# Routed expert results in a vision tower: three accumulators in DRAM, or one row per pick and token

## The reference

```python
h = h + _L1_ffn_ref(_layernorm(h, axis=-1), Wg, bg, Wge, bge, W1, b1, W2, b2)

# inside _L1_ffn_ref: G, E = 4, 8 (32 experts); KG, KE = 2, 2 (four picks per token)
comb = _combine_weights(xf, Wg, bg, Wge, bge)          # (tokens, 32), four non-zero each
h = gelu(einsum('nd,edm->nem', xf, W1) + b1)           # M = 768
y = einsum('nem,emd->ned', h, W2) + b2
out = einsum('ne,ned->nd', comb, y)
```

## Time and profile before

| | us |
|---|---|
| median of 3 runs | 1153.36 |
| lowest, highest | 1148.75, 1153.44 |
| the profiled execution | 1146.11 |
| its span, first to last instruction | 1144.3 |
| TensorE matmuls busy in it | 1015.9 |
| VectorE, ScalarE, GpSimd busy | 403.2, 671.7, 232.7 |

### The profile page before, as it was taken

The page is one execution under the profiler, slowest core; times in us unless marked ns, Lnnn a source line. Parts: engine busy times, 40 slices in busy tenths (PEclk is TensorE's granted clock), DMA queues, the critical chain, the costliest instruction groups (busy, mean ns, idle before and its releaser), DMA issues. The chain is left out here.

```text
span 1144.3 us, 22007 instructions
## 1 busy us (share of the span) xinstructions
PE 1015.9 (89%) x7432; PEld 668.2 (58%) x7432; DVE 403.2 (35%) x1027; ACT 671.7 (59%) x1227; POOL 232.7 (20%) x236
## 2 busy tenths in 40 slices
PE   8879689989999999999999998873299999999992
PEld 7455456633444444444445454452189999999992
DVE  2666968750111111111111115767822222222220
ACT  0657957679988888888788852451033433343330
POOL 0110310000000000000000000200655555555532
PEclk9999889989999999999999998896589999999997
DMA  9200037979555445455444401004199999999994
GB/s 278 79 2 0 1 125 262 340 270 172 120 117 134 111 114 127 95 124 124 112 111 117 106 1 46 0 6 129 49 326 313 311 307 306 309 309 307 304 288 73
DMA packets 72411, 183.74 MB, mean 161 GB/s; under 512 B 15712, under 2 KB 30400, under 8 KB 72008
## 3 DMA queue, kind: packets, MB, share of 16 engines
q1 hardware_dynamic: 59260, 166.24, 48.7%
q0 software_dynamic: 12640, 16.16, 7.1%
q10 hardware_dynamic: 432, 0.26, 0.1%
HBM read 147.52 MB, written 36.67 MB: 161 GB/s over the span
## 5 line engine op out<-in xcount | busy, mean ns | idle before, releaser
L1145 ACT ACTIVATE sle_H<-sle_hp 128x1024 f32<-128x1024 f32 x384 | 367.5, 1024 | 61.1 <-PE sle_hp L1082 61.1
L1565 ACT ACTIVATE ext_H<-ext_hp,ext_bias 128x128 f32<-128x128 f32 x378 | 104.3, 375 | 171.9 <-issue 153.8
L1099 PE MATMUL sle_up<-sle_H,sle_cw 128*32 128x512 f32 (+1 forms) x2048 | 193.5, 496 | 0.0
L1523 PE MATMUL ext_yp<-ext_w,ext_H 128*128 128x192 f32 x756 | 139.7, 335 | 2.2 <-ACT ext_H L1565 1.6
L1160 DVE STREAM_TRANSPOSE sle_UT<-sle_up 128x256 f32<-128x256 f32 x64 | 37.3, 583 | 295.1 <-PE sle_up L1099 295.1
L1523 PEld LDWEIGHTS ext_yp<-ext_w,ext_H 128*128 128x128 f32 x756 | 121.1, 190 | 10.0 <-issue 2.6
L1082 PE MATMUL sle_hp<-keep_G,keep_dT 99*128 99x512 bf16 (+1 forms) x512 | 103.6, 337 | 10.9 <-PEq L880 5.7
L1099 PEld LDWEIGHTS sle_up<-sle_H,sle_cw 128*32 128x32 f32 x2048 | 53.8, 109 | 87.6 <-issue 74.2
L1082 PE MATMUL sle_hp<-sle_G,sle_dT 99*128 99x512 bf16 (+1 forms) x512 | 99.9, 327 | 1.1 <-ACT sle_H L1145 1.1
L1067 POOL COPY sle_cw<-keep_CT 128x128 f32 (+1 forms) x64 | 18.7, 293 | 396.1 <-PE sle_up L1099 396.0
L1508 PE MATMUL ext_hp<-ext_xT,ext_w 128*128 128x128 f32 x756 | 96.1, 277 | 0.0
(11 more groups left out here) (258 smaller groups left out, 1158.2 us busy)
## 6 DMA issues: line engine op xcount, KB each, us to landing
ext_w<-W SPq DMA_DIRECT2D x126, 576.0 KB
pieces<-hid_gp SPq DMA_DIRECT2D x16, 1152.0 KB, 4.9
keep_G<-pieces SPq DMA_DIRECT2D x32, 288.0 KB, 3.9
sle_G<-pieces SPq DMA_DIRECT2D x32, 288.0 KB, 3.8
pieces<-hid_gp SPq DMA_DIRECT2D x8, 768.0 KB, 4.7
keep_G<-pieces SPq DMA_DIRECT2D x32, 192.0 KB, 3.8
sle_G<-pieces SPq DMA_DIRECT2D x32, 192.0 KB, 3.7
keep_CT<-xT SPq DMA_DIRECT2D x6, 512.0 KB, 6.2
```

Source lines behind the costliest of these rows:

```text
L1099: mm = pe.matmul(to[32 * e:32 * e + 32], cw[:, p, 2 * e + grp, :], H[:, p, h:h + width], start=(p == 0 and grp == 0), stop=(p == 1 and grp ...
L1145: act.activation(H[:, p, WIDTH * k:WIDTH * (k + 1)], hp[k % DEEP][:].rearrange("p a c -> p (a c)"), ACT.Gelu_apprx_tanh).then_inc(gelu_don ...
L1523: mm = pe.matmul(yp[:, 0:D], H[:, q, c, :], w2[:, q, c, :], start=(c == 0), stop=(c == HC - 1))
L1565: act.activation(H[:, q, c, :], hp[q][:, c % 2, (c // 2) * P:(c // 2 + 1) * P], ACT.Gelu, bias=bias[:, q, c:c + 1]).then_inc(gelu_done, 1)
```

## The change

The three tensors with additions are replaced by one DRAM tensor `chosen` of 4 * 1024 + 128 rows, in which each (pick, token) pair has its own row.

- `route` no longer zeroes `sum1` and `sum2`. `rt.slot` is unchanged, but the third number of it is no longer read.
- SP no longer stores h to `out` at the start.
- Each scatter is plain, goes to `chosen` at the pair's number (`rt.slot[:, 1]`), and waits for the landing of the scatter before it, tile t - 1. All use one semaphore, `y_out`. `leave_y` waits for the same scatter as before, that of tile t - 3, by that semaphore's count.
- The merges go. When all 63 scatters have landed, SP loads `chosen` back in eight pieces, two halves of the tokens by four picks, each 128 x 4 x 192, into `back`. VectorE adds each piece to h, and SP stores each half of h to `out` when its four are added.

```diff
-            sp.wait_ge(zero_ready, 1)
-            for rows in others:
-                sp.dma_start(rows.rearrange("(i p) d -> p i d", p=P), zero[:].unsqueeze(1).to_broadcast([P, TILES + 1, D])).then_inc(zero_out, 16)
...
-            sp.wait_ge(zero_out, 16 * len(others))
...
-            pool.memset(zero[:], 0.0).then_inc(zero_ready, 1)
...
-                if first and p == DEEP - 1:
-                    sp.wait_ge(h_done, TILES // 2)
-                    sp.dma_start(out[0:TOKENS].rearrange("(i p) d -> p i d", p=P), g.h[:]).then_inc(first_out, 16)
-                    sp.dma_start(out[TOKENS:TOKENS + P], g.h[:, 0, :]).then_inc(first_out, 16)
 
             program(sp, load)
+            rows = lambda dram: dram.rearrange("(i p) d -> p i d", p=P)
+            sp.wait_ge(y_out, 16 * MOE_TILES)
+            for half in range(2):
+                at = slice(half * TILES // 2, (half + 1) * TILES // 2)
+                for k in range(TOPK):
+                    sp.dma_start(back[:, k, at], rows(chosen[k * TOKENS:(k + 1) * TOKENS])[:, at]).then_inc(back_in[half][k], 16)
+            for half in range(2):
+                at = slice(half * TILES // 2, (half + 1) * TILES // 2)
+                sp.wait_ge(total, TOPK * (half + 1))
+                sp.dma_start(rows(out[0:TOKENS])[:, at], g.h[:, at]).then_inc(total_out, 16)
+            sp.wait_ge(total_out, 32)
...
-                dve.tensor_copy((xi, yi)[n][q][:], rt.slot[:, 2 * n, bass.ds(t, 1)]).then_inc((xi_ready, yi_ready)[n], 1)
+                dve.tensor_copy((xi, yi)[n][q][:], rt.slot[:, n, bass.ds(t, 1)]).then_inc((xi_ready, yi_ready)[n], 1)
...
-                    dve.wait_ge(y_out[q], 16 * uses(p, r))
+                    dve.wait_ge(y_out, 16 * (t - DEEP + 1))
...
             leave_y(MOE_TILES - 1, BODY - 1, ROUNDS - 1, False)
+            for half in range(2):
+                at = slice(half * TILES // 2, (half + 1) * TILES // 2)
+                for k in range(TOPK):
+                    dve.wait_ge(back_in[half][k], 16)
+                    dve.tensor_tensor(g.h[:, at], g.h[:, at], back[:, k, at], ALU.add).then_inc(total, 1)
+                    dve.wait_ge(total, TOPK * half + k + 1)
...
-            def scatter(t, p, r, first, last):
-                q = p % DEEP
-                to = 0 if last and p >= BODY - DEEP else q
+            def scatter(t, p, start):
                 pool.wait_ge(yi_ready, t + 1)
                 pool.wait_ge(y_done, t + 1)
-                if first:
-                    pool.wait_ge(first_out, 32)
-                else:
-                    pool.wait_ge(y_out[to], 16 * (uses(p, r) + q - to))
+                if not start:
+                    pool.wait_ge(y_out, 16 * t)
                 pool.sem_inc(turn, 1)
-                pool.indirect_dma_start(out=sums[to], out_offset=bass.IndirectOffsetOnAxis(ap=yi[q][:], axis=0),
-                                        in_=y[:, q, :], in_offset=None, compute_op=ALU.add).then_inc(y_out[to], 16)
-
-            def merge(into, q):
-                whole = lambda rows: rows[0:TOKENS].rearrange("(p i) d -> p (i d)", i=4)
-                pool.dma_start(whole(sums[into]), whole(sums[q]), accum_op=ALU.add, max_dma_last_dim=4 * 4 * D).then_inc(merged, 16)
+                pool.indirect_dma_start(out=chosen, out_offset=bass.IndirectOffsetOnAxis(ap=yi[p % DEEP][:], axis=0),
+                                        in_=y[:, p % DEEP, :], in_offset=None).then_inc(y_out, 16)
...
-                    scatter(t - 1, (p - 1) % BODY, r + (p - 1) // BODY, first and p <= DEEP, last and p > 0)
-                if last and p == BODY - DEEP + 1:
-                    for q in range(1, DEEP):
-                        pool.wait_ge(y_out[q], 16 * (MOE_TILES // DEEP - 1))
-                    merge(1, 2)
+                    scatter(t - 1, (p - 1) % BODY, first and p == 1)
 
             for q in range(BODY):
                 gather(q, q)
             program(pool, tile)
-            scatter(MOE_TILES - 1, BODY - 1, ROUNDS - 1, False, True)
-            pool.wait_ge(merged, 16)
-            pool.wait_ge(y_out[0], 16 * (MOE_TILES // DEEP + DEEP - 1))
-            merge(0, 1)
-            pool.wait_ge(merged, 32)
+            scatter(MOE_TILES - 1, BODY - 1, False)
+            pool.wait_ge(y_out, 16 * MOE_TILES)
...
-        others = [nc.dram_tensor(f"sum{i}", (TOKENS + P, D), F32).ap() for i in range(1, 3)]
-        route(nc, g, a, rt, xn_dram, others)
-        expert_tiles(nc, g, a, rt, xn_dram, out, others)
+        chosen = nc.dram_tensor("chosen", (TOPK * TOKENS + P, D), F32).ap()
```

More of the change, by code:

```diff
@@ L1203, with route @@
     pass
-def route(nc, g, a, rt, xn_dram, others):
+def route(nc, g, a, rt, xn_dram):
     SETS = TILES * G1 + TILES
@@ L1231, in route @@
         lg = s.sb("lg", [P, TILES, G1 + EXPERTS])
-        zero = s.sb("zero", [P, D])
         val = s.sb("val", [P, SETS, E1])
@@ L1256, in route @@
                                "in_ready", "step"))
-        zero_ready, zero_out = s.sem("zero_ready"), s.sem("zero_out")
         xn_out, row_ready, owner_ready, owner_out, slot_done, gate_ready, gate_out = (
@@ L1422, in _, with expert_tiles @@
             dve.wait_ge(slot_done, 2)
-def expert_tiles(nc, g, a, rt, xn_dram, out, others):
+def expert_tiles(nc, g, a, rt, xn_dram, out, chosen):
     DEEP, BODY = 3, 9
     ROUNDS = MOE_TILES // BODY
-    sums = [out, *others]
     with Scope(nc, "ext") as s:
@@ L1442, in expert_tiles @@
         shareT = s.sb("shareT", [P, 2, P])
+        back = s.sb("back", [P, TOPK, TILES, D])
         xi = [s.sb(f"xi{i}", [P, 1], U32) for i in range(BODY)]
@@ L1449, in expert_tiles @@
                                "gelu_done", "y_ready", "y_done", "turn", "step"))
-        share_ready, shareT_done, b2_ready, h_done, first_out, merged = (
-            s.sem(n) for n in ("share_ready", "shareT_done", "b2_ready", "h_done", "first_out", "merged"))
-        y_out = [s.sem(f"y_out{i}") for i in range(DEEP)]
+        share_ready, shareT_done, b2_ready, h_done, y_out, total, total_out = (
+            s.sem(n) for n in ("share_ready", "shareT_done", "b2_ready", "h_done", "y_out", "total", "total_out"))
+        back_in = [[s.sem(f"back_in{half}_{k}") for k in range(TOPK)] for half in range(2)]
         w1_in, w2_in = ([s.sem(f"{n}{i}") for i in range(DEEP)] for n in ("w1_in", "w2_in"))
@@ L1683, in routed_moe @@
         xn_dram = nc.dram_tensor("xn", (TOKENS, ROW), F32).ap()
-        others = [nc.dram_tensor(f"sum{i}", (TOKENS + P, D), F32).ap() for i in range(1, 3)]
-        route(nc, g, a, rt, xn_dram, others)
-        expert_tiles(nc, g, a, rt, xn_dram, out, others)
+        chosen = nc.dram_tensor("chosen", (TOPK * TOKENS + P, D), F32).ap()
+        route(nc, g, a, rt, xn_dram)
+        expert_tiles(nc, g, a, rt, xn_dram, out, chosen)
 def build(nc, a, out):
```

## The result

The changed kernel takes 1183.06 us (median of 4 runs, 1174.18 to 1188.97), the kernel before in the same series 1151.05 us (4 runs, 1145.57 to 1153.44). The ratio is 1.028, with a 95% interval from 1.023 to 1.033: slower by 2.8%. The time lies in the forecast's range of 1147 to 1195, but the likeliest case, 1155 and no change, was wrong. It is rival B in its mild form, which stood at 1181. The range reached up to 1195 in order to hold that rival, so the time's place in it says nothing for the mechanism that was forecast.

The account below looks back on a forecast made before the run. TensorE was taken to set the pace, 4.57 us a tile. Loop terms summed to 0 and the end to +1.4 us; on the three runs' median of 1153.36 us that gave 1154.8, rounded 1155, range 1147 to 1195.

Parts of the forecast that it names:

- the likeliest case: Whole kernel: the scatter chain fits the tile period and the ends cancel; 1155 us, from 1152 to 1160, chance 0.46.
- rival B: GpSimd's wait for scatter t-1 binds the tile loop from a landing of 3.70 us on; chances 0.26 mild, 0.12 strong.
- mild form: Tile loop: a landing of 4.1 us makes a loop of 5.0, +26 us, 1181 us; 1160 to 1195, chance 0.26.
- What bounds the kernel: Routed tile loop: TensorE sets the pace at 4.57 us a tile; DMA engines just keep up, cheaper transfers give nothing.
- Zeroing and stores of h: In `route` and at the routed stage's start: removing zeroing is worth 0, removing stores of h 0, at most -1 us.
- The chain: Tile loop: each scatter waits for the one before; landing plus 0.87 against 4.57 us, sum 0, bounds 0 and +134 us.
- a late scatter moves itself: Tile loop: a late scatter slides against weight loads until it falls behind the burst or in the gap, landing in about 3 us.
- The gap: Tile loop: plain scatters leave the DMA engines 0.65 us free in each 4.57 us period, a load of 86%.
- strong form: Tile loop: landing of 5.2 us, loop of 6.1, price 90 us, 1245 us; over 1195, chance 0.12.
- The end: Behind the last matmul: merges go, eight loads, adds and stores come; span ends at 1145.7 against 1144.3, +1.4 us, between -1 and +6.
- The open 4.3 us: End of the span before: 4.3 us after the second merge landed, unexplained; 0.6 taken for the new end, 4.3 kept as bound.
- rival D: End is longer: the eight loads don't run at 317 GB/s, or the 4.3 us stay; 1161 us, chance 0.05 beyond 1159.

Follow-up runs that it names:

- light weights: Changed kernel, chain kept, with half of each W2 left out of its load (down product reads three of six chunks twice): 1156.0 us, one run.

## Why the prediction was right and where it was wrong

**What bounds the kernel: right.** TensorE sets the pace before, and cheaper transfers give nothing in the loop: plain scatters alone leave the period at 4.57 us.

**Zeroing and stores of h: not contradicted.** They were put at 0 and -1 us at most. The 1.06 us less from the first gather to the first `y` is within what that stretch varies by (16.6 to 20.4 us), so these runs can't tell it from 0.

**The chain: the form of the sum was right, the choice of its value was the step that failed.** The loop is landing plus 0.81 us (I had 0.87; outside the hardware loop over the tiles it is 0.88 to 0.90 here too), so it binds from a landing of 3.76 us on, and the scatter and then `leave_y` wait as I had it. The last link was wrong: TensorE waits not for `leave_x` and x transposed but for `leave_y` to free `yp`, before its down product. That changes no number. The bounds, 0 and 134 us, held the 27.3 us. The failed step reads "I take the low part of it, a loop that just fits, for one reason: a late scatter moves itself". What the runs show in its place: a late scatter did move against the weight loads, and settled in no place where it lands in about 3 us. In the changed kernel the first eight loops, while TensorE still kept its own pace, were 4.35 to 7.66 us, 6.0 in the mean; with nine buffers 28 tiles passed that way at 5.9 us a loop. The loop came down to 5.0 us only once TensorE waited for the chain: slower tiles and so fewer weights, perhaps also a fixed order between the two. I didn't have this feedback, and what needs TensorE to wait can't end at 4.57 us. The gap on which I relied was also smaller: 0.09 of a period (share 0.91 without a chain), not 0.14.

I had two rows of landings beside load, 5.21 and 5.9 us, and an idle one of 3.52, and for a loop in which the engines are 86% busy I took a value from the idle end. By the fit of the Trainium skill, in "DMA: Bandwidth & Descriptors" (Anatomy of one DMA), an estimate for this scatter is 2.2 us. The idle rows agree, 2.3 us; in the loop it is 4.2. The same page of the Trainium skill (Latency and other measured facts) has the fixed cost grow with the load of HBM, which was the sentence beside rival B, and the rows go the same way, 2.3 us to 4.2; that HBM is the cause no run here shows.

**Rival B: right in mechanism and, for the loop, in size.** It had a landing of 4.1 us, a loop of 5.0 and 26 us; measured 4.2, 5.0 and 27.3. That its total, 1181, is so near to 1183 is partly luck: it stood on 1153.4 us before, and the end cost 5.3 us more than it held. The reason that kept its strong form unlikely, that slower tiles fill less of the engines, was just the feedback: I used it to cap the loss and not to see that it also holds the loop above the period.

**The end: +1.4 predicted, +6.65 measured.** By its terms:

| term | predicted | measured |
|---|---|---|
| last `y` to the issue of the last scatter | 2.2 | 6.8 |
| its landing | 2.9 | 2.3 |
| the loads, to the last piece in SBUF | 11.7 | 13.3 |
| last add | 1.0 | 1.0 |
| last store | 2.9 | 2.6 |
| block end | 0.6 | 0.4 |

The first is the chain once more, three scatters to drain at 3.21 us; without a chain the last scatter is issued 1.2 us after the last `y`. Less the fixed 1.7 us of the prediction, the loads took 11.6 us for 3.15 MB, 271 GB/s, where I had taken 317 from stores; the end of them ran beside the first store. The open 4.3 us of before did not stay: they were GpSimd's drain at the end of its block, 3.9 us in the trace of before, and that now runs beside SP's loads. So of rival D the slower loads came, with 1.6 us, and the 4.3 us did not.

**The checks that the prediction named.** DMA share 0.86 to 0.9: 0.87, but for the wrong reason, the tiles being longer. A plain scatter in 2.9 us at the end: 2.3. Eight loads in 11.6: 13.3. Last matmul to end of span 21.4: 26.6. The period above 4.57 us is what it said would make the prediction wrong.

## What to carry to other kernels

A wait for the transfer just issued puts a whole landing into every round; ask for the loaded landing, and take it from a row where the same queue ran beside the traffic of that loop, not from the idle end of the kernel. If the landing plus the step to the next issue doesn't fit into the period, look for the shortest wait that does: here, with rows of their own for the spare lanes, waiting for the transfer before that one was free. More buffers don't repair a chain that is slower than its producer. With four and six they only moved the loss to the drain, and with nine what was queued on the same engine came too late.

## What was not expected of the hardware

- A scatter's landing is that of the slowest of 16 engines. In the loop of the changed kernel (means of tiles 9 to 49) the first packet of a scatter moves 1.96 us after the issue (1.55 with idle engines), and by the semaphore events the middle one of the 16 engines is done at 3.16 us and the last at 4.21; alone they are done at 2.23 and 2.33. So half of what the load adds is the spread between engines. The Trainium skill states in "DMA: Bandwidth & Descriptors" (Why a DMA increments its semaphore by 16 and not by 1) that each engine posts its own increment, and the events here are such.
- An adding scatter is dearer than a plain one of the same bytes in three places: 1.59 to 0.99 us of GpSimd's time to issue, 3.4 to 3.5 us to land alone against 2.3, and 0.4 us of the 16 engines in each tile (share 1.00 to 0.91).
- Where the hardware loop over the tiles is left, at tile 54, one period of the changed kernel is 8.49 us, and the next 4.02; the chain of waits has 3.87 us there in which nothing was waited for that the profile shows. No period of the kernel before is longer than 4.81. With light weights a step of 7.46 us between two scatters falls near that place too, and no period there is longer than 4.78. Whatever the pause is, a chain without slack passes it on. It wasn't taken apart.
